# A four-layer cross-attention and feed-forward chain: extra constant products on TensorE, down products ten steps behind, and a split wait

## The chip, the cores and the metric

The kernel runs on one core of a Trainium2 chip. The metric is the time of one execution on the device in microseconds (us), as the median of several runs. Five engines work side by side, each through its own list of instructions in the order in which they were written: TensorE (PE, matrix products into PSUM), VectorE (DVE), ScalarE (ACT), GpSimd (POOL) and SyncE (SP, which here only starts DMAs). Semaphores order them against each other.

## The reference, cut to what matters

The input x is 4 batches of 256 tokens of width 256; a context of 4 times 64 tokens of width 64 is given too. Everything is float32, with a tolerance that makes the kernel split its operands into a high and a low float16 part in many places. Each layer adds a cross-attention and a feed-forward part to x, both of them on a normed x:

```
x = x + L0_xattn(layernorm(x), ctx)    # 16 heads of 16, causal, latent keys and values
x = x + L0_ffn(layernorm(x))           # one value projection, width 704, routed by a sign
x = x + L1_xattn(layernorm(x), ctx)    # folded head weights, rotated queries and keys
x = x + L1_ffn(layernorm(x))           # 64 experts of 64 (top 8) and a shared one
x = x + L2_xattn(layernorm(x), ctx)    # folded head weights, not rotated
x = x + L2_ffn(layernorm(x))           # self-attention, 8 experts of 176 (top 2), shared 704
x = x + L3_xattn(layernorm(x), ctx)    # as L0_xattn
x = x + L3_ffn(layernorm(x))           # 16 experts of 176 (top 4), shared 176
```

An expert part is `down(silu(gate(x)) * up(x))` times its gate; the kernel computes all experts for all tokens and multiplies by gates that are zero for those not chosen.

## The kernel before

The 1024 tokens are 8 tiles of 128 (`NT`). The stages follow each other in each engine's list in the order of the blocks at the end of `build`: latent attention 0, pre-work 0 and feed-forward 0, folded attention 1, router 1 and feed-forward 1, folded attention 2, self-attention with router 2 and feed-forward 2, latent attention 3, router 3 and feed-forward 3. No planner sets the order: it is written out by loops with offsets, and whatever PE waits for holds everything that follows it in PE's list.

**Constant products.** `pe_warm(n, free)` (L303, its product is L306) issues n products of the constant `ident_b` with the constant mask, 128 by 128 by 512 in bfloat16, into a PSUM bank that nothing reads. They have no effect on the result. The kernel before has them in several places already.

**Latent attention** (`pe_latent`, used for layers 0 and 3). Eight sets of heads run through scores (L419, mask L422), softmax on DVE and ACT, transposes (L430), values (L440), the transposed reciprocals (`inverse`, L449) and the output projection (`output`, L458), in a loop over m that has each step some turns behind the one before.

**Pre-work 0** (`pe_pre0`): transposes of z (L299), the folded projection (L1811), constants, then transposes of z2, which DVE writes in L1909.

**Folded attention 1** (`pe_rotated`): 48 units of queries (L1052 to L1054) and scores (L1066), and for each of the four batches four groups of transposes (L1076) and two outputs (L1084). After the last unit only the last batch's transposes and outputs are left; they wait for DVE, POOL (L1142) and ACT (L1115).

**Folded attention 2** (`pe_fold2`): eight pairs of heads, each with `folded` (L861), `chained` (L871), `values` (L883), `queries` (L890), `pe_fold_values` (L679) and `pe_keys2` (L922). Before the first stands the wait for the whole x of feed-forward 1 (`x_ready(pe, 2 * n)`).

**Self-attention** (`pe_self`): 32 steps; in each `turned` (L2236) transposes the exponentials of ACT (L2313) after waiting for them (`s.p`) and for DVE's copy of the turned block before (`s.pt`, L2329), then come scores two steps ahead, and the values. `project` (L2267) ends each group of four.

**Feed-forward** (`pe_ffn`, `act_ffn`, `dve_ffn`, `pool_ffn`, `sp_ffn`): the hidden width goes in steps, two for each tile of 128 columns (512 tokens each). In a step PE computes gate and up, six products each (L1450 to L1452); ACT takes the tanh, DVE forms the product into `m_b`, POOL multiplies the gate rows in (L1697), ACT and DVE split the product in high and low (L1604, L1651), and `LAG` steps later PE's `down` (L1495 to L1497, twelve products) takes it. `LAG` is 8, and it is also the number of slots of `m_b`. In the last `LAG` steps there are only down products left (`in_order`). The gate values come from the router: DVE ends them in L1997, PE transposes them (`gates_turned`, L1482) in step 3, ACT copies them in its step 4, SP writes them to memory and reads them back as rows (`m_g`). The weight tiles come by SP through two buffers each; a down tile is split by `act_dn_hi` and `dve_dn_lo`.

## Time and profile before

| what | value |
|---|---|
| median of 3 runs | 1262.36 us |
| the 3 runs | 1260.95, 1262.36, 4173.52 us |
| the profiled execution | 1260.15 us |
| its span | 1258.0 us |
| mean granted clock of TensorE in it | 0.981 |
| instructions in it | 21685 |

The span is the time from the first to the last instruction that the profile holds; the 2.15 us around it belong to the execution but to no row. One of the three runs took 4173.52 us; the other two lie 0.8 and 2.2 us above the profiled execution. In the rows, the granted clock is given as a share of full speed: 1.00 is 2.4 GHz, 0.50 is 1.2 GHz.

### The profile page before, as it was taken

To read this page: it belongs to the slowest core of one execution; us is meant where nothing else is said; L and a number is where in the kernel's file an instruction comes from. 1 tells how busy PE (TensorE), PEld (TensorE's weight loads), DVE (VectorE), ACT (ScalarE), POOL (GpSimd) and SP (SyncE) were. 2 spreads that over 40 slices of the span, in tenths; PEclk is the share of its full clock that TensorE was granted. 3 is DMA by queue.
4 is the path that set the end of the run, shared out by engine and by line. 5 is a ranking of instruction groups with operands and counts; after the bars stand their busy time and mean duration, and the time that the engine had idled before them with its cause. 6 is when DMAs were issued, how large, how long until landed. Compare 5 with 4: busy or idle time off the path is not lost.

```text
span 1258.0 us, 21685 instructions
## 1 busy us (share of the span) xinstructions
PE 1172.4 (93%) x8429; PEld 770.3 (61%) x8429; DVE 922.1 (73%) x1718; ACT 507.8 (40%) x1141; POOL 395.2 (31%) x397
## 2 busy tenths in 40 slices
PE   6988999999889999999999988889999988899998
PEld 3664657999645556565666745554666665455556
DVE  3677976767567777778757797887778576677777
ACT  3433361111124333333453336653334343555554
POOL 1450124666305333334102340002533142433331
PEclk9799999999999999999999999999999989999999
DMA  4040132000055444445140000002433100443441
GB/s 148 1 160 18 39 124 75 1 1 2 1 195 155 118 117 118 117 118 137 53 178 1 1 17 2 2 2 72 140 118 118 56 18 1 124 118 117 118 127 63
DMA packets 41541, 97.17 MB, mean 77 GB/s; under 512 B 5446, under 2 KB 18246, under 8 KB 39392
## 3 DMA queue, kind: packets, MB, share of 16 engines
q1 hardware_dynamic: 41440, 95.79, 25.0%
q8 instruction: 67, 1.10, 0.4%
q14 instruction: 34, 0.28, 0.1%
HBM read 94.35 MB, written 1.42 MB: 76 GB/s over the span
## 4 chain that ended last, share of the span: by engine, by line
PE 74%; DVE 16%; ACT 4%; issue 2%; DMA 2%; POOL 1%; SPq 0%; DVEq 0%; ACTq 0%; POOLq 0%
PE PS L1450 9%; PE PS L1451 9%; PE PS L1452 9%; PE PS L1495 5%; PE PS L1497 5%; PE PS L1496 4%; PE PS L1066 3%; PE PS L1084 2%; PE PS L1261 2%; PE PS L306 2%; ACT arena L2313 2%; PE PS L1052 2%; PE PS L1054 2%; PE PS L1053 2%; DVE arena L1651 2%
## 5 line engine op out<-in xcount | busy, mean ns | idle before, releaser
L1697 POOL TENSOR_TENSOR arena<-arena,m_g 128x512 f32<-128x512 f32 x142 | 198.3, 1417 | 361.2 <-DMA m_g<-gate_rows 314.8
L1450 PE MATMUL PS<-arena 128*128 128x512 f16 x608 | 231.5, 381 | 2.9 <-DVE arena L1637 2.4
L1451 PE MATMUL PS<-arena 128*128 128x512 f16 x608 | 231.3, 380 | 0.0
L1452 PE MATMUL PS<-arena 128*128 128x512 f16 x608 | 231.0, 380 | 0.0
L1495 PE MATMUL PS<-arena 128*128 128x256 f16 x608 | 165.9, 273 | 8.0 <-DVE arena L1651 6.6
L1497 PE MATMUL PS<-arena 128*128 128x256 f16 x608 | 165.8, 273 | 0.0
L1496 PE MATMUL PS<-arena 128*128 128x256 f16 x608 | 165.7, 273 | 0.0
L1594 ACT ACTIVATE arena<-PS 128x512 f32<-128x512 f32 x112 | 66.8, 597 | 229.2 <-PE PS L1452 227.5
L1640 DVE SCALAR_TENSOR_TENSOR arena<-arena,PS 128x512 f32<-128x512 f32 x112 | 76.9, 687 | 80.6 <-ACT arena L1594 78.8
L1651 DVE TENSOR_TENSOR arena<-arena 128x512 f16<-128x512 f32 x142 | 132.0, 931 | 2.9 <-ACT arena L1604 2.8
L1452 PEld LDWEIGHTS PS<-arena 128*128 128x128 f16 x608 | 59.7, 98 | 72.3 <-issue 1.1
L1450 PEld LDWEIGHTS PS<-arena 128*128 128x128 f16 x608 | 59.7, 98 | 62.7 <-DVE arena L1637 2.9
L1451 PEld LDWEIGHTS PS<-arena 128*128 128x128 f16 x608 | 59.7, 98 | 57.7 <-issue 0.6
L1135 POOL TENSOR_TENSOR arena<-arena 128x256 f32<-128x256 f32 x96 | 67.7, 728 | 79.2 <-DVE arena L1165 79.1
L1604 ACT ACTIVATE arena<-arena 128x512 f16<-128x512 f32 x142 | 87.6, 618 | 5.3 <-PE PS L1497 4.2
L1643 DVE TENSOR_TENSOR arena<-arena,PS 128x512 f32<-128x512 f32 x112 | 77.1, 688 | 12.2 <-DVE arena L1640 0.5
L1495 PEld LDWEIGHTS PS<-arena 128*128 128x128 f16 x608 | 59.4, 98 | 38.5 <-issue 10.2
L1539 DVE SCALAR_TENSOR_TENSOR arena<-w_stage,arena 128x512 f16<-128x512 f32 x80 | 79.2, 992 | 4.9 <-ACT arena L1534 4.9
L1496 PEld LDWEIGHTS PS<-arena 128*128 128x128 f16 x608 | 59.5, 98 | 17.0
L1497 PEld LDWEIGHTS PS<-arena 128*128 128x128 f16 x608 | 59.5, 98 | 6.9
L2313 ACT ACTIVATE arena<-PS,arena 128x128 f32<-128x128 f32 (+1 forms) x128 | 52.1, 422 | 20.4 <-DVE arena L2085 19.9
L1637 DVE TENSOR_TENSOR arena<-arena,PS 128x512 f32<-128x512 f32 x44 | 30.2, 686 | 37.5 <-PE PS L1452 37.2
(282 smaller groups left out, 2250.5 us busy)
## 6 DMA issues: line engine op xcount, KB each, us to landing
w_stage<-in_up SPq DMA_DIRECT2D x80, 256.0 KB, 2.8
m_g<-gate_rows SPq DMA_DIRECT2D x70, 256.0 KB, 4.2
arena<-in_heads SPq DMA_DIRECT2D x16, 1088.0 KB, 5.5
w_stage<-in_down SPq DMA_DIRECT2D x80, 128.0 KB, 4.0
m_g<-gate_rows SPq DMA_DIRECT2D x17, 512.0 KB, 4.1
m_g<-gate_rows SPq DMA_DIRECT2D x6, 448.0 KB, 4.0
m_g<-gate_rows SPq DMA_DIRECT2D x6, 384.0 KB, 4.0
m_g<-gate_rows SPq DMA_DIRECT2D x6, 320.0 KB, 4.5
```

The costliest lines, as they stand in the source:

```text
L1450: pe.matmul(to, w_hi, x_hi, start=(k == 0), stop=False)
L1451: pe.matmul(to, w_lo, x_hi, start=False, stop=False)
L1452: ins = pe.matmul(to, w_hi, x_lo, start=False, stop=(k == KT - 1))
L1495: pe.matmul(to, h_hi, w_hi, start=(c == 0 and i % 2 == 0), stop=False)
L1496: pe.matmul(to, h_hi, w_lo, start=False, stop=False)
L1497: ins = pe.matmul(to, h_lo, w_hi, start=False, stop=(last and i % 2 == 1))
L1539: nc.vector.scalar_tensor_tensor(up_w[:, c % 2, 1, :], up_in[:, c % 2, :], SPLIT, up_w[:, c % 2, 0, :], ALU.mult, ALU.subtract).then_inc(s ...
L1604: act.activation(hid_part(n, 0, st), m_b[:, st % LAG, :], ACT.Copy).then_inc(s.hi, 1)
L1643: dve.tensor_tensor(m_b[:, st % LAG, :], a, u_ps, ALU.mult).then_inc(s.prod, 1)
L1651: dve.tensor_tensor(hid_part(n, 1, st), m_b[:, st % LAG, :], hid_part(n, 0, st), ALU.subtract).then_inc(s.lo, 1)
L1697: pool.tensor_tensor(p, p, m_g[:, st // 2 % 2, st % 2, :], ALU.mult).then_inc(s.c, 1)
L2313: ins = act.activation(sa_p[:, t % 2, e, a * keys:(a + 1) * keys], PS[:, score_banks(t), a * keys:(a + 1) * keys][:, e, :], ACT.Exp, bias= ...
```

## The change

It consists of these edits. `LAG` becomes 10. In latent attention 4, 5 and 3 constant products come ahead of the loop and in its steps m = 2 and m = 3; `inverse(b)` comes behind the wait and the 4 constants that followed it; behind the last `inverse` come 6 constants (layer 0) or 16 (layer 3). In folded attention 2 the products of `folded(0)` come first, then a wait for x tile 5 alone, the first `pe_fold_values`, 4 constants; the wait for the whole x comes behind `chained(0)`, and 6 constants and the old wait go. At the end of folded attention 1, 3, 3, 11 and 3 constants come ahead of the last four groups of transposes, and 9 become 6 ahead of the output. In feed-forward 1 the gates are transposed in step 4 in place of 3, behind 5 constants, and ACT copies them in step 5; a down tile is no longer split for the first of two due steps where that one is odd. In pre-work 0, 13 constants become 28. In self-attention the wait for `s.pt` comes first, then 3 constants (t = 2, 6, 10, ..., 30) or 4 (t = 1 and 4), then the wait for `s.p`; 6 more stand ahead of the last `project`.

```diff
@@ -34,7 +34,7 @@
 UNDOWN = 1.0 / (HID * SPLIT)
 UP_W, DN_W = 4 * P, D
-LAG = 8
+LAG = 10
 HIDS = 4
 RING = 4
@@ -466,7 +466,10 @@
             scores(0)
             projected(1, 1)
+            pe_warm(4, LAT_Y)
             for m in range(1, SETS + 3):
+                if m in (2, 3):
+                    pe_warm(5 if m == 2 else 3, LAT_Y)
                 if m % 2 and m >= 3:
                     for q in range(QT):
@@ -480,11 +483,13 @@
                 if m % 2 and m >= 3:
                     b = (m - 3) // 2
-                    inverse(b)
                     if b < B - 1:
                         if n or b:
                             pe.wait_ge(soft.x, NT * n + 2 * b)
                         pe_warm(4, LAT_Y)
+                    inverse(b)
+                    if b == B - 1:
+                        pe_warm(16 if n else 6, LAT_BANK[0])
                 if m % 2 == 0 and m >= 4:
                     output((m - 4) // 2, 1)
@@ -897,13 +902,18 @@
                     ins.then_inc(ln.xT_ps, 1)
 
-            pe.wait_ge(*heads_loaded(2, 0))
+            folded(0)
+            x_ready(pe, 4, 5)
             pe_fold_values(6, 0).then_inc(s.e_ps, 1)
+            pe_warm(4, 0)
             for q in range(PAIRS):
-                folded(q)
+                if q:
+                    folded(q)
                 if q:
                     pe_keys2(q - 1)
                 chained(q)
+                if q == 0:
+                    x_ready(pe, 4)
                 values(q)
                 queries(q)
@@ -1011,8 +1021,6 @@
                 pe_rotated()
             else:
-                pe_warm(6, 3)
-                x_ready(pe, 2 * n)
                 pe_fold2()
                 pe_plain()
@@ -1092,11 +1100,13 @@
                 for e in range(4):
                     if at_turn(g, TURN_AT[e]) is not None:
+                        if g >= UNITS:
+                            pe_warm((3, 3, 11, 3)[e], 4)
                         transposed(at_turn(g, TURN_AT[e]), e)
                 for q in range(QT):
                     if at_turn(g, OUT_AT[q]) is not None:
                         if g >= UNITS and q == 0:
-                            pe_warm(9, 4)
+                            pe_warm(6, 4)
                         output(at_turn(g, OUT_AT[q]), q)
 
@@ -1372,6 +1382,9 @@
         def slot_load(s, kind, c):
             return {"up": (s.up0, s.up1), "dn": (s.dn0, s.dn1)}[kind][c % 2]
+
+        def gates_at(n):
+            return 4 if n == 1 else 3
 
         def gated(n, st):
@@ -1477,6 +1490,8 @@
 
             def gates_turned():
+                if n == 1:
+                    pe_warm(5, 6)
                 pe.wait_ge(s.parts, n)
                 for i in range(NT):
@@ -1519,7 +1534,7 @@
                 if st == 0 and n:
                     pe_logits(n, 1)
-                if st == 3 and f.gated:
+                if st == gates_at(n) and f.gated:
                     gates_turned()
                 if st == LAG and f.gated:
@@ -1608,13 +1623,14 @@
             for st in range(f.steps + LAG - 2):
                 c, h, due = st // 2, st % 2, finished(n, st)
-                if st == 4 and f.gated:
+                if st == gates_at(n) + 1 and f.gated:
                     act.wait_ge(s.gates_ps, n)
                     to_hid = HID * 0.5 * UNSPLIT * (1.0 if f.first else UNSPLIT)
                                    scale=to_hid).then_inc(s.gates, 1)
                 if len(due) == 2:
-                    act_dn_hi(n, due[0] // 2)
+                    if due[0] % 2 == 0:
+                        act_dn_hi(n, due[0] // 2)
                     high(due[0])
                 if begun <= st < f.steps:
@@ -1656,7 +1672,8 @@
                 c, h, due = st // 2, st % 2, finished(n, st)
                 if len(due) == 2:
-                    dve_dn_lo(n, due[0] // 2)
+                    if due[0] % 2 == 0:
+                        dve_dn_lo(n, due[0] // 2)
                     low(due[0])
                 if begun <= st < f.steps:
@@ -1812,7 +1829,7 @@
                 if i % 2:
                     ins.then_inc(s.y_ps, 1)
-            pe_warm(13, 3)
+            pe_warm(28, 3)
             pe_transpose_tiles(z, s.z2, 0, s.z2T_ps, BY_HALF)
             pe_warm(5, 4)
@@ -2227,9 +2244,11 @@
             def turned(t):
                 b, q, j0, keys = sa_part(t)
-                pe.wait_ge(s.p, t + 1)
                 if t:
                     pe.wait_ge(s.pt, t)
+                    if t % SA_OF_Q == 2 or t in (1, 4):
+                        pe_warm(3 if t % SA_OF_Q == 2 else 4, 2)
+                pe.wait_ge(s.p, t + 1)
                 for e in range(2):
                     for a in range(2):
@@ -2281,6 +2300,7 @@
             values(SA_STEPS - 2)
             sums_transposed(B * QT - 1)
+            pe_warm(6, 2)
             project(B * QT - 1)
 
```

## Rows read from the trace of the kernel before

**Rows 1.** The page: busy time by engine, and the chain that ended last.
```profile
PE 1172.4 (93%) x8429; PEld 770.3 (61%) x8429; DVE 922.1 (73%) x1718; ACT 507.8 (40%) x1141; POOL 395.2 (31%) x397
...
PE 74%; DVE 16%; ACT 4%; issue 2%; DMA 2%; POOL 1%; SPq 0%; DVEq 0%; ACTq 0%; POOLq 0%
```

**Rows 2.** Stretches: span, busy of PE, PEld, DVE, ACT, POOL, PE clock, DMA, GB/s.
```profile
32.60:49.70 17.10, 15.10 (x103) 11.46 (x102) 10.60 (x17) 7.66 (x13) 8.07 (x14) 0.50 0.01 1
100.60:104.60 4.00, 3.55 (x17) 3.51 (x18) 3.72 (x12) 2.37 (x6) 0.01 (x1) 0.57 0.00 0
336.50:340.00 3.50, 3.40 (x11) 1.76 (x12) 2.30 (x6) 1.59 (x3) 0.00 (x0) 0.51 0.00 0
367.30:370.90 3.60, 3.00 (x12) 2.26 (x13) 1.13 (x3) 0.99 (x1) 0.00 (x0) 0.53 0.25 74
752.40:756.00 3.60, 3.58 (x15) 1.31 (x16) 3.56 (x8) 0.11 (x1) 0.00 (x0) 0.58 0.00 0
1012.50:1023.00 10.50, 9.81 (x73) 7.33 (x74) 6.91 (x12) 4.62 (x8) 4.47 (x8) 0.52 0.10 27
1053.30:1056.80 3.50, 3.50 (x15) 2.95 (x14) 2.12 (x7) 0.59 (x2) 0.00 (x0) 0.51 0.02 5
1090.50:1094.10 3.60, 3.60 (x14) 1.58 (x12) 1.87 (x3) 1.06 (x3) 1.94 (x3) 0.55 0.93 255
```

**Rows 3.** PE's waits over the span: us in total, times, longest us.
```profile
PE PS L458 <- DVE arena L591: 7.1, 6, 4.2
...
PE PS L1495 <- DVE arena L1651: 6.6, 10, 2.0
```

**Rows 4.** Timeline of PE, constant products: start us, us, instruction, count.
```profile
47.54 1.91 PE L306 MATMUL PS<-causal_b,ident_b 128*128 128x512 bf16 x4
...
93.93 2.97 PE L306 MATMUL PS<-causal_b,ident_b 128*128 128x512 bf16 x13
```

**Rows 5.** Timeline of PE in latent attention 0 and 3; in brackets idle before, and releaser.
```profile
35.31 1.11 PE L430 MATMUL PS<-ident,arena 128*128 128x128 f32 x4 [1.32 <-ACT arena L520]
36.36 2.08 PE L419 MATMUL PS<-arena 32*128 32x128 f32 x16
...
50.92 1.16 PE L419 MATMUL PS<-arena 32*128 32x128 f32 x16
...
61.25 1.16 PE L419 MATMUL PS<-arena 32*128 32x128 f32 x16
...
1010.53 1.16 PE L419 MATMUL PS<-arena 32*128 32x128 f32 x16
...
1024.15 1.16 PE L419 MATMUL PS<-arena 32*128 32x128 f32 x16
...
1052.40 2.92 PE L458 MATMUL PS<-arena 128*128 128x256 f32 x8 [4.21 <-DVE arena L591]
```

**Rows 6.** Timeline of PE, then of DVE, where pre-work 0 ends.
```profile
101.05 3.58 PE L299 MATMUL PS<-ident,arena 128*128 128x128 f32 x16 [4.15 <-DVE arena L1909]
...
100.64 2.19 DVE L1909 TENSOR_SCALAR arena<-arena,rms_r 128x256 f32<-128x256 f32 x8 [1.76 <-POOL rms_r L1836]
```

**Rows 7.** Timeline of PE at the end of folded attention 1.
```profile
335.17 0.66 PE L1076 MATMUL PS<-ident,arena 128*128 128x128 f32 x4 [2.94 <-POOL arena L1142]
...
337.48 3.32 PE L306 MATMUL PS<-causal_b,ident_b 128*128 128x512 bf16 x9
```

**Rows 8.** Timeline of PE where feed-forward 1 and 3 begin.
```profile
367.90 1.97 PE L1482 MATMUL PS<-ident,arena 128*65 128x128 f32 x8 [4.45 <-DVE arena L1997]
...
384.30 0.27 PE L1495 MATMUL PS<-arena 128*128 128x256 f16 x1 [1.03 <-DVE arena L1651]
...
1089.63 0.27 PE L1495 MATMUL PS<-arena 128*128 128x256 f16 x1 [2.04 <-DVE arena L1651]
```

**Rows 9.** Timeline of PE where folded attention 2 begins.
```profile
620.13 1.10 PE L871 MATMUL PS<-arena 96*128 96x64 f32 x8 [0.47 <-ACT arena L957]
```

**Rows 10.** Timeline of PE in self-attention, steps 10 and 14.
```profile
784.68 0.66 PE L2236 MATMUL PS<-ident,arena 128*128 128x128 f32 x4 [0.78 <-ACT arena L2313]
...
795.72 1.06 PE L2236 MATMUL PS<-ident,arena 128*128 128x128 f32 x8 [0.96 <-DVE arena L2329]
```

## The prediction

> **What bounds the kernel now.** I read the page first: TensorE (PE) is busy for 93% of the span and holds 74% of the chain that ended last [rows 1]. So what counts is what PE does, how fast its clock lets it, and the 86 us (1258.0 - 1172.4) in which it stands. Then I cut the span into slices of half a microsecond and looked for a granted clock under 1.00. It is low in eight stretches [rows 2]; the share of a stretch at the half level (1.2 GHz) is twice what is missing from 1.00: 17.1, 3.4, 3.4, 3.4, 3.0, 10.1, 3.4 and 3.2 us, 47 us in all. PE is busy for 45.5 us of them, so a clock that never fell would give back at most 23 us. Last I read PE's waits [rows 3] and its timeline around each place that the diff touches. Ahead of each low stretch PE stood for microseconds or did short work between waits: 4.15 us before 101.05 [rows 6], 2.94 before 335.17 [rows 7], 4.45 before 367.90 and 2.04 before 1089.63 [rows 8], 4.21 before 1052.40, and 1.32 before 35.31 [rows 5].
>
> The sum is made against the profiled execution, 1260.15 us, which is 2.2 us under the median; the next run of before is 0.8 us above it. I add 1.5 us at the end.
>
> **Constant products.** Thirteen at full clock take 2.97 us and four at half clock 1.91; the last one of each has to drain, so one more costs 0.216 us or 0.427 us (the difference of neighbours' starts) [rows 4]. One that stands in a wait is free if it ends before the wait does; if not, all that is behind it in PE's list is later by the rest.
>
> *Latent attention, layers 0 and 3.* At full clock the loop needs 10.33 us for two steps of m (50.92 to 61.25). The two before took 14.56 in layer 0 (36.36 to 50.92) and 13.62 in layer 3 (1010.53 to 1024.15) [rows 5], most of it at half clock [rows 2]. If the added products hold the clock, 4.2 and 3.3 us go. The work of the steps is the same, so the row nearest to the new stretch is the loop at full clock; a few tenths are lost again by the `inverse` that now stands behind four constants (0.86 us, most of it in a wait that it had for POOL: an estimate). The five products at m = 2 are 1.08 us and fit in the 1.32 us before 35.31. I take -4.0 + 0.2 and -3.3 + 0.3. If the clock falls all the same, the twelve cost 12 x 0.427 = 5.1 us against some 3.3 us of waits: +1.8 us for each layer. In layer 3 the last wait is 4.21 us [rows 5]; 16 products are 3.46 us and are hidden, the transposes and outputs of 1053.3 to 1056.8 are at half clock now [rows 2], and half of 3.4 us is 1.7: I take -1.5 (0 to -1.7). The six in layer 0 (1.3 us) stand in a wait of the same kind (one of six, 7.1 us in all [rows 3]): 0.
>
> *Pre-work 0.* 28 products from 93.93 end at 93.93 + 28 x 0.216 = 100.0, within PE's wait until 101.05 [rows 4, 6]. The sixteen transposes behind it take 3.58 us at half clock; at full clock they would follow DVE, whose eight writes end at 102.83 [rows 6], and end some 1.4 us earlier. DVE then still has its splitting to do, which PE's next products wait for, so less than that arrives: -0.9 (0 to -1.5).
>
> *End of folded attention 1.* The eleven products are 2.37 us in the wait of 2.94 us [rows 7]: hidden. The three ahead of the first group stand in no wait and delay the chain by up to 0.65 us; part of it is lost in waits of ACT, I take 0.25. Behind, six at full clock (1.3 us) replace nine that took 3.32 us at half clock, and a group of transposes speeds up by 0.4 us: 0.25 - 2.0 - 0.4 = -2.1. If the clock falls earlier, eleven cost 4.7 us in a wait of 2.94: up to +2.4.
>
> *Self-attention.* 8 x 3 + 2 x 4 = 32 products, 6.9 us. In step 10 the wait is for ACT (0.78 us) and the copy of the block before is done by its start: three products (0.65 us) are hidden. In step 14 the wait of 0.96 us is for that copy itself (L2329), and the constants stand behind it: 0.65 us late [rows 10]. Steps 10, 18 and 26 are of the first kind, 14, 22 and 30 of the second, and I count 2 and 6 with these. A later wait of PE for ACT takes up a part; I take 0.4 for each of the five: +2.0 (0 to +6.9). The clock was 1.00 in this stretch, so there is nothing to win. The six ahead of the last `project`: 0.
>
> **Down products ten steps behind.** The number of products is the same. What changes is the start: ten steps of up products (12 x 0.216 = 2.6 us each) run before the first down product, 5.2 us more than with eight. In feed-forward 3 PE waited 2.04 us for the first down operand, because the gate rows arrive late, and the clock then fell for 3.2 us [rows 2, 8]: 2.0 + 1.6 = -3.6 (0 to -3.7). Feed-forward 2 has a small wait of the same kind: of the 6.6 us in ten waits for L1651 [rows 3], 3.1 us are named here, and I take 0.7 of the rest: -0.7. At the ends ten down products run in a row in place of eight, and with them the down tiles have to come one after the other through two buffers: +0.3 (0 to +2). Feed-forward 0 has only 11 steps; nearly all its down products now come behind all up products, where DVE's splitting and its work for the routing set the pace: +0.5 (-0.5 to +2).
>
> *Feed-forward 1* also has its gates a step later. PE stands 4.45 us, until DVE's gates are there, and the transposes take 1.97 us, mostly at half clock [rows 8]. Now the products of step 4 come first; they need the next weight tile, which DVE splits only behind the gates, so PE stands 0.6 us longer. Then come step 4 (the clock low until 370.9 as before [rows 2]), five constants (1.08 us) in no wait at all, and the transposes at full clock, 1.0 in place of 1.8 us: 0.6 + 1.08 - 0.8 + 0.4 for the products that take the half clock in the transposes' place = +1.3. The 1.03 us before 384.30 [rows 8] should go: the transposes end some 4.4 us later (about 374.3 in place of 369.9), and the first down product comes 5.2 + 1.3 us later. But the margin is thin, I take +0.8 (0 to +3).
>
> **Second fold.** Six constants (1.3 us), the wait for x and the folded values came before the products of `folded(0)`; ACT's copy of these ended the wait at 620.13 [rows 9]. Now `folded(0)` runs while DVE still adds x, and ACT's copies follow some 0.8 us earlier: -0.8 (0 to -1.3).
>
> **Sum:** latent attention -3.8 - 3.0 - 1.5, pre-work -0.9, folded attention 1 -2.1, self-attention +2.0, feed-forward 0 to 3 +0.5 + 0.8 - 0.7 - 3.6, ends +0.3, second fold -0.8: -12.8. 1260.15 - 12.8 + 1.5 = 1248.9 us.
>
> **The skill against it.** The clock is at the half level for 47 of 1258 us [rows 2], 3.7% of the span, and giving it all back would be 1.9%. The Trainium skill ("TensorE: Matmul & The Clock Gate", "What's actually happening") says that the ramp costs under 1% of a typical kernel's span and that the number of slow products changes from run to run. By its 1% the clock part of my sum (4.2 + 3.3 + 1.5 + 0.9 + 2.4 + 1.6 = 13.9 us) would be 12.6 us at most, and the result 1250.2. The rows show more than that for this kernel. The second half of the rule is rival B, whose price comes from rows.
>
> **The rivals.**
> A. *The constants are not hidden in self-attention and in the latent loops.* For it: step 14's wait is DVE's [rows 10], and PE's queue is in order. Price: self-attention 32 x 0.216 = 6.9; latent attention +1.8 + 1.8 at half clock; folded attention 1 +2.4; feed-forward 1 +1.6; with the gains that don't hang on it (-0.9 - 1.5 - 0.8 - 4.3 + 0.8): +7.8, so 1269 us. It decides from the point where a constant outlasts the wait: 1.32 us holds six at full clock and three at half. Against it: most waits are longer than what is put in.
> B. *The clock falls elsewhere.* The stretch at 752.4 lies in code that isn't changed ahead of it, and whether a wait lowers the clock depends on more than its length: 4.21 us and 2.04 us did [rows 5, 8], the 1.03 us before 384.30 did not [rows 2, 8], so a wait in between may do so once it has moved. If the latent loops fall back for half of their length (+3.6) and two new stretches of 3.4 us come (+3.4), the result is 1256 us.
> C. *More than I count.* No cost in self-attention, none at the ends, and the stretches at 367.3 and 752.4 go too (-3.1): 1249 - 2 - 3.1 - 1.3 = 1242.5 us.
> D. *LAG does nothing for the starts.* If POOL and the gate rows set the pace, the wait before the first down product only moves: without -3.6, -0.7 and the 1.03 us, 1254 us.
>
> **How the numbers follow.** Forecast 0.45, A 0.12, B 0.22, C 0.11, D 0.10. Its own range is 1244 to 1253; with B, C and D whole and part of A 1240 to 1262. A measurement of this kernel can tell 2% (25 us) from no change: under 1237 us there would have to be more than all the clock gives, over 1287 us more than A. Faster by over 2%: 0.04, slower: 0.02, within: 0.94.
>
> **What would show it.** Right: the granted clock 1.00 between 28 and 60 us, at 101, 337, in both ends of latent attention 3 and behind the first down product of feed-forward 3; no wait before the first down products; two steps of the latent loop in 10 to 11 us from m = 2; self-attention 2 us longer; the gates of feed-forward 1 transposed some 6 us later. Wrong: half-clock stretches in the latent loops (B), constants with DVE and ACT idle beside them in self-attention (A), a wait before the first down product (D).

## The result, and the profile after

| | median (fastest to slowest) | ratio to before, 95% interval |
|---|---|---|
| before, 6 runs beside it | 1260.81 us (1259.71 to 4173.52) | |
| after, 6 runs | 1252.97 us (1250.47 to 1255.29) | 0.9933 (0.9911 to 0.9954) |
| after, profiled | 1252.46 us, span 1250.4 us, mean granted clock 0.996 | |

One run of before (4173.52 us) and one of e7 below (6432.05 us) stand far outside the others; the ratios and e7's range leave them out.

The forecast was 1249 us with a range of 1240 to 1262 us, a gain of 1.1% on the median before; measured is a gain of 0.7%, with the time near the upper end of the forecast's own narrow range (1244 to 1253). The sum itself (1247.4 us for the profiled execution) missed by 5.1 us, and that is two errors against each other: the four feed-forwards came out 9.8 us worse than in the sum, all the rest 4.7 us better. That the time lies so near the forecast is in part luck.

Line numbers in the rows of a run are those of its own kernel. In the changed kernel the gate product L1450 is L1463, the down product L1495 is L1510, the DVE split of the product, L1651 (L1653 in feed-forward 0), is L1667 (L1669), the product L1637 is L1653, and the split of an up tile, L1539, is L1554. The page of the changed kernel, the lines of [rows 1]:

```profile
PE 1179.2 (94%) x8519; PEld 767.1 (61%) x8548; DVE 918.0 (73%) x1718; ACT 505.3 (40%) x1141; POOL 391.4 (31%) x397
...
PE 72%; DVE 16%; DMA 3%; ACT 3%; issue 3%; POOL 2%; SPq 1%; DVEq 0%; ACTq 0%; POOLq 0%
```

PE is busy for 6.8 us more in a span that is 7.6 us shorter: the added constants are in it, and the waits and the half clock are what went. Stretches of the changed kernel, with the columns of [rows 2]:

```profile
28.00:60.00 32.00, 28.53 (x299) 20.02 (x303) 24.65 (x42) 17.39 (x31) 16.67 (x28) 1.00 0.01 2
361.00:368.00 7.00, 5.30 (x12) 1.94 (x14) 2.26 (x6) 1.11 (x2) 0.00 (x0) 0.51 0.13 37
752.40:756.00 3.60, 2.79 (x20) 1.20 (x18) 2.46 (x6) 2.51 (x11) 0.00 (x0) 1.00 0.00 0
1012.00:1023.00 11.00, 10.07 (x115) 7.43 (x112) 8.48 (x16) 5.94 (x11) 5.93 (x11) 1.00 0.01 3
1064.00:1068.00 4.00, 3.66 (x13) 1.69 (x14) 2.27 (x4) 1.28 (x4) 0.00 (x0) 0.57 0.29 66
```

Of the 47.8 us at half clock ahead of the last products, 10.2 are left (6.8 at 361 and 3.4 at 1064). The latent loops run at 1.00 throughout. PE's timeline in them, at the end of latent attention 3, at the end of pre-work 0 and at the end of folded attention 1 (the places of [rows 5], [rows 6] and [rows 7]):

```profile
34.43 1.16 PE L419 MATMUL PS<-arena 32*128 32x128 f32 x16
...
45.15 1.16 PE L419 MATMUL PS<-arena 32*128 32x128 f32 x16
...
1045.88 2.00 PE L458 MATMUL PS<-arena 128*128 128x256 f32 x8 [0.76 <-DVE arena L596]
...
88.38 5.99 PE L306 MATMUL PS<-causal_b,ident_b 128*128 128x512 bf16 x27
95.29 2.27 PE L299 MATMUL PS<-ident,arena 128*128 128x128 f32 x16 [0.91 <-DVE arena L1926]
...
328.01 2.54 PE L306 MATMUL PS<-causal_b,ident_b 128*128 128x512 bf16 x11
...
332.37 1.46 PE L306 MATMUL PS<-causal_b,ident_b 128*128 128x512 bf16 x6
```

Two steps of the loop that took 14.56 us take 10.72 (34.43 to 45.15). The wait of 4.21 us before the last outputs holds 16 constants and 0.76 us of idle time, and the eight outputs take 2.00 us in place of 2.92. The sixteen transposes of pre-work 0 take 2.27 us in place of 3.58.

PE's waits over the span, with the columns of [rows 3]:

```profile
PE PS L1463 <- DVE arena L1554: 6.1, 1, 6.1
PE PS L1510 <- DVE arena L1667: 6.0, 11, 1.2
PE PS L306 <- DVE arena L2349: 5.5, 9, 1.1
PE PS L458 <- DVE arena L596: 4.5, 8, 0.8
...
PE PS L1463 <- DVE arena L1653: 2.9, 2, 2.4
```

The down products (L1510, L1495 before) still wait 6.0 us for L1667, against 6.6 us, now in eleven waits: no long one, and hardly less in all. In feed-forward 1 one wait of 6.1 us stands where 4.45 us stood [rows 8]. PE's timeline there:

```profile
362.58 0.61 PE L1463 MATMUL PS<-arena 128*128 128x512 f16 x1 [6.10 <-DVE arena L1554]
...
368.01 1.03 PE L306 MATMUL PS<-causal_b,ident_b 128*128 128x512 bf16 x4
368.88 1.04 PE L1497 MATMUL PS<-ident,arena 128*65 128x128 f32 x8
...
390.57 0.28 PE L1510 MATMUL PS<-arena 128*128 128x256 f16 x1 [1.21 <-DVE arena L1667]
```

Step 4's products now come first. They wait for DVE's split of the third weight tile, and PE's list holds nothing else: the five constants stand behind this wait, not in it. The clock falls, all twelve products of step 4 run at half clock (362.58 to 367.9, 5.3 us in place of 2.6), and the constants come when there is nothing left to cover. DVE's timeline shows why the wait is longer than the 0.6 us that the forecast added: the split follows the sums of the gates in its list.

```profile
359.48 0.68 DVE L2010 TENSOR_TENSOR arena<-arena 128x512 f32<-128x512 f32 x1
360.20 0.69 DVE L2011 TENSOR_REDUCE arena<-arena 128x8 f32<-128x512 f32 x1
...
361.84 0.68 DVE L1554 SCALAR_TENSOR_TENSOR arena<-w_stage,arena 128x512 f16<-128x512 f32 x1
```

The lengths of the stages, each from its first to its last product in the two traces, in us against before:

| stage | predicted | after | the same kernel profiled again |
|---|---|---|---|
| latent attention 0 up to the loop; the loop | 0; -3.8 | -1.3; -4.5 | -0.8; -4.4 |
| pre-work 0 | -0.9 | -1.1 | -1.1 |
| feed-forward 0 | +0.5 | +2.2 | +2.2 |
| end of folded attention 1 | -2.1 | -2.3 | -2.3 |
| feed-forward 1 | +0.8 | +5.4 | +2.0 |
| second fold | -0.8 | -1.0 | -1.0 |
| self-attention | +2.0 | -0.3 | +1.4 |
| feed-forward 2 | -0.7 | -0.8 | +0.7 |
| latent attention 3 | -4.5 | -4.3 | -4.4 |
| feed-forward 3 | -3.6 | +0.3 | -0.3 |

(The predicted +0.3 for the ends is not placed.) The last column is e5 below. The same program differs by 3.4 us in feed-forward 1, where the clock was low for 3.4 us in place of 6.8 and PE stood 1.8 us less, and by 1.7 us in self-attention, where a stretch of 3.4 us at 748 is in the one trace and not in the other. So the length of a single stage is good to the clock's luck in it. The end of folded attention 1, pre-work 0, the second fold, feed-forward 0 and latent attention 3, which have no low stretch, agree to 0.1 us. Feed-forward 2 has none either and differs by 1.5 us: there it is waits, 0.3 us for L1667 in the one trace and 1.9 us in the other.

### The profile page after: what moved, and what is told of

It reads as the page before. It is cut to its first block, busy times and chain, and to the rows that moved or that the text cites. A ratio compares the mean times of both kernels' runs of the same rounds, so it can differ in the third digit from the quotient of the medians.

```text
span 1250.4 us, 21883 instructions
## 1 busy us (share of the span) xinstructions
PE 1179.2 (94%) x8519; PEld 767.1 (61%) x8548; DVE 918.0 (73%) x1718; ACT 505.3 (40%) x1141; POOL 391.4 (31%) x397
## 4 chain that ended last, share of the span: by engine, by line
PE 72%; DVE 16%; DMA 3%; ACT 3%; issue 3%; POOL 2%; SPq 1%; DVEq 0%; ACTq 0%; POOLq 0%
PE PS L1463 8%; PE PS L1465 8%; PE PS L1464 8%; PE PS L1510 5%; PE PS L1512 5%; PE PS L1511 5%; PE PS L1074 3%; PE PS L1092 2%; PE PS L306 2%; PE PS L1271 2%; DMA w_stage<-in_up 2%; PE PS L1060 2%; PE PS L1062 2%; PE PS L1061 2%; PE PS L2255 1%
## 5 line engine op out<-in xcount | busy, mean ns | idle before, releaser
L1714 POOL TENSOR_TENSOR arena<-arena,m_g 128x512 f32<-128x512 f32 x142 | 194.8, 1391 | 359.9 <-DMA m_g<-gate_rows 351.0
L1463 PE MATMUL PS<-arena 128*128 128x512 f16 x608 | 232.1, 382 | 9.6 <-DVE arena L1554 6.1
L1510 PE MATMUL PS<-arena 128*128 128x256 f16 x608 | 165.9, 273 | 9.1 <-DVE arena L1667 6.0
L1667 DVE TENSOR_TENSOR arena<-arena 128x512 f16<-128x512 f32 x142 | 125.4, 887 | 2.2 <-ACT arena L1619 1.8
L1463 PEld LDWEIGHTS PS<-arena 128*128 128x128 f16 x608 | 59.7, 98 | 71.4 <-DVE arena L1554 6.6
L1659 DVE TENSOR_TENSOR arena<-arena,PS 128x512 f32<-128x512 f32 x112 | 77.0, 688 | 13.7 <-PE PS L1465 1.5
L1554 DVE SCALAR_TENSOR_TENSOR arena<-w_stage,arena 128x512 f16<-128x512 f32 x80 | 81.6, 1022 | 7.0 <-ACT arena L1549 7.0
L1510 PEld LDWEIGHTS PS<-arena 128*128 128x128 f16 x608 | 59.4, 98 | 39.1 <-DVE arena L1667 10.7
L306 PE MATMUL PS<-causal_b,ident_b 128*128 128x512 bf16 x235 | 57.6, 379 | 7.3 <-DVE arena L2349 5.5
```

The lines of the kernel that those rows point to most:

```text
L306: nc.tensor.matmul(PS[:, free, :], ident_b[:], mask_lat, start=True, stop=True)
L1463: pe.matmul(to, w_hi, x_hi, start=(k == 0), stop=False)
L1510: pe.matmul(to, h_hi, w_hi, start=(c == 0 and i % 2 == 0), stop=False)
L1554: nc.vector.scalar_tensor_tensor(up_w[:, c % 2, 1, :], up_in[:, c % 2, :], SPLIT, up_w[:, c % 2, 0, :], ALU.mult, ALU.subtract).then_inc(s ...
L1659: dve.tensor_tensor(m_b[:, st % LAG, :], a, u_ps, ALU.mult).then_inc(s.prod, 1)
L1667: dve.tensor_tensor(hid_part(n, 1, st), m_b[:, st % LAG, :], hid_part(n, 0, st), ALU.subtract).then_inc(s.lo, 1)
```

## Experiments

All ratios are against before on the same chip. "Half clock" is the time at 1.2 GHz ahead of the last products, from the granted clock of half-microsecond stretches. The other columns are the stage's length against before's trace.

| run | median us (range) | ratio (95%) | half clock | ffn 0 | ffn 1 | ffn 2 | ffn 3 |
|---|---|---|---|---|---|---|---|
| before | | | 47.8 | | | | |
| e1 | 1248.95 (1247.8-1249.9) | 0.9879 (.9857-.9902) | 10.2 | 0.0 | +2.6 | 0.0 | +0.4 |
| e2 | 1249.47 (1247.9-1250.8) | 0.9883 (.9860-.9907) | 6.8 | +2.2 | +0.7 | -0.1 | -1.5 |
| e3 | 1252.17 (1248.8-1255.6) | 0.9902 (.9875-.9930) | 17.1 | 0.0 | +5.2 | +0.6 | +1.5 |
| e4 | 1263.43 (1260.8-1271.2) | 1.0003 (.9983-1.0023) | 47.8 | +2.2 | -1.7 | +0.8 | +3.0 |
| e5 | 1251.71 (1250.3-1253.1) | 0.9918 (.9899-.9936) | 10.2 | +2.2 | +2.0 | +0.7 | -0.3 |
| e6 | 1254.54 (1252.9-1256.7) | 0.9942 (.9923-.9961) | 17.1 | +2.2 | +2.8 | +1.1 | +1.8 |
| e7 | 1264.44 (1255.0-1267.3) | 1.0014 (.9993-1.0036) | 37.5 | +2.2 | +3.5 | -0.6 | +4.4 |
| e8 | 1245.65 (1244.6-1247.6) | 0.9872 (.9851-.9892) | 6.8 | 0.0 | +0.1 | +0.6 | 0.0 |
| e9 | 1247.61 (1244.0-1250.5) | 0.9876 (.9849-.9903) | 6.8 | +2.2 | -1.4 | +1.8 | +0.5 |
| e10 | 1244.58 (1243.3-1246.1) | 0.9856 (.9826-.9886) | 3.4 | 0.0 | -1.5 | -0.8 | -0.3 |
| e11 | 1247.60 (1245.5-1248.7) | 0.9877 (.9850-.9904) | 3.4 | +2.2 | -1.0 | -0.7 | -1.3 |
| e12 | 1245.85 (1244.9-1246.7) | 0.9865 (.9835-.9894) | 3.4 | 0.0 | +0.7 | +1.0 | -2.2 |

(Before's medians on the three chips were 1263.9, 1262.1 and 1263.8 us.)

### The feed-forward edits taken back, alone and together (e1 to e4)

**e1**: the changed kernel with all of its feed-forward edits taken back. **e2**: only the gates' step and its constants back. **e3**: only the distance back. **e4**: the kernel before with the distance of ten alone (and, as the change has it, a down tile split once and not twice where two steps are due).

The distance (e1, e3), then the gates (e1, e2):

```diff
-LAG = 10
+LAG = 8
```

```diff
-            return 4 if n == 1 else 3
+            return 3
...
-                if n == 1:
-                    pe_warm(5, 6)
```

> The changed kernel with LAG back at 8 and the gates of feed-forward 1 back in step 3 without the five constants; all other constants and the split wait stay. Theory (the feed-forward edits cost what the constants win): feed-forward 0 takes 2.2 us less than in the changed kernel, feed-forward 1 some 4 to 5 less, feed-forward 2 0.8 more, so 1246 us (1244 to 1248). Rival (the feed-forward stages lost by the place where the clock fell and by a late weight tile, whatever LAG is): the wait ahead of step 4 of feed-forward 1 stays at 6 us with 6.8 us at half clock, and the time stays at 1251 to 1253 us.

> The changed kernel with LAG 10, but the gates of feed-forward 1 in step 3 again and without the five constants ahead of them. Theory (the gate step costs by itself: the constants in no wait, and twelve products at half clock where transposes were): feed-forward 1 is 2 to 3 us shorter, 1250 us. Rival (the gate step is free, the loss is LAG's): within 1 us of the changed kernel, 1252 to 1254 us.

> The changed kernel with LAG 8, the gates of feed-forward 1 still in step 4 behind five constants. Theory: feed-forward 0 takes back its 2.2 us, but in feed-forward 1 the gate rows now come too late for a first down product after eight steps: PE waits 4 to 6 us there, so 1252 to 1255 us. Rival (the gates have slack enough): the wait stays at 1 us and the time is 1248 to 1250 us.

> The kernel before with LAG 10 alone. Theory (LAG alone wins nothing): feed-forward 0 +2.2 us, feed-forward 1 about 0 (its 1 us wait moves to the second down product, where the up tile arrives late), feed-forward 2 -0.8, feed-forward 3 between -1.6 and 0: 1260 to 1262 us. Rival (my forecast: the waits ahead of the first down products go): -3.5 us, 1257 us.

Measured: e1 and e2 lie 2 to 4 us under the changed kernel's two medians (1252.97 and 1251.71), 0.4 to 0.5% by the ratios, and do not differ from each other. e1 is 1 us over the range expected. So the constants and the second fold give 15 us on their own (1263.88 - 1248.95), 1.2%, and with the feed-forward edits 0.7 and 0.8% are left: they take a third or more of it away.

The distance of ten alone does nothing for the time (e4, 1.0003); in place of the gain of up to 1.6 us expected for feed-forward 3, e4's trace has a loss of 3.0. The traces divide the rest. Feed-forward 0 is 2.16 or 2.17 us longer in each of the eight traces with ten steps there and within 0.01 us of before in each of the five with eight. PE's waits at its end, of the changed kernel:

```profile
131.86 0.27 PE L1510 MATMUL PS<-arena 128*128 128x256 f16 x1 [0.79 <-DVE arena L1669]
133.84 0.27 PE L1510 MATMUL PS<-arena 128*128 128x256 f16 x1 [0.51 <-DVE arena L1669]
135.82 0.27 PE L1510 MATMUL PS<-arena 128*128 128x256 f16 x1 [0.51 <-DVE arena L1669]
137.80 0.27 PE L1510 MATMUL PS<-arena 128*128 128x256 f16 x1 [0.51 <-DVE arena L1669]
```

Each down step follows the one before by 1.98 us, DVE's pace with the routing in it, where PE would need 1.5. There are two more such steps behind the last up product: from there to the end it is 18.7 us in place of 14.8, and ahead of it the stage is only 1.7 us shorter. In feed-forward 1 the distance gains 1.5 to 1.9 us, since its wait before the first down product goes (e1 against e2, e8 against e9). The two cancel.

The gates a step later cost 2.6 us with eight steps (e3 against e1, both with 6.8 us of half clock there) and up to 4.7 us with ten (the changed kernel against e2). In e3 PE waits 1.76 us before the first down product, not the 4 to 6 us expected.

Feed-forward 1 is 2.6 us longer than before in e1 too, where none of its edits is left. The wait for the gates is 5.22 us there in place of 4.45 [rows 8], and the low stretch behind it 6.8 us in place of 3.4:

```profile
359.89 1.97 PE L1495 MATMUL PS<-ident,arena 128*65 128x128 f32 x8 [5.22 <-DVE arena L2012]
```

The gates' transposes begin 17.0 us after the first product of the stage (16.9 to 17.1 in all six traces with the gates in step 3 behind the changed end of folded attention 1), 16.2 in before: PE is 2.3 us quicker through that end, and 0.8 us of it is lost again in this wait. So a part of the changed kernel's +5.4 us hangs on no edit of this stage. Why the low stretch is twice as long is not shown; in e5, behind a wait of 5.71 us, it is 3.4 us again.

### The changed kernel again, and without its constants (e5 to e7)

**e5** is the changed kernel. **e6** leaves out those of self-attention, **e7** those added in the two latent stages.

```diff
-                    if t % SA_OF_Q == 2 or t in (1, 4):
-                        pe_warm(3 if t % SA_OF_Q == 2 else 4, 2)
...
-            pe_warm(6, 2)
```

```diff
-            pe_warm(4, LAT_Y)
...
-                if m in (2, 3):
-                    pe_warm(5 if m == 2 else 3, LAT_Y)
...
-                    if b == B - 1:
-                        pe_warm(16 if n else 6, LAT_BANK[0])
```

> The changed kernel itself once more, on the chip of the next three runs, as their ground. Every theory: 0.993 of the time before (1252 to 1255 us), feed-forward 0 2.2 us longer than before, feed-forward 1 about 5.4 us longer, half clock for some 7 us ahead of the products of feed-forward 1's step 4 and for some 3 us in feed-forward 3.

> The changed kernel without the 38 constant products in self-attention. Theory one (constants that fill waits keep the clock up and pay wherever the clock would fall): self-attention loses the 1.4 us which the constants cost there, but the half-clock stretch at its start (before: 752.4 to 756, some 1.6 us of loss) comes back, net within 0.5 us either way of the changed kernel. Rival (they are pure cost there): 1.4 us faster, with no half-clock stretch. Second rival (they hold the clock up further on): the clock falls in several further places of self-attention or of the stages behind it, 2 to 4 us slower.

> The changed kernel without the constants added in the latent stages 0 and 3 (the changed order of the inverse stays). Theory one (the constants there are what took the half-clock stretches of 17 and 10 us away): latent 0 is 5 to 6 us longer than in the changed kernel, latent 3 3 to 4 us longer, with half clock in both, 9 us in all, so 1261 to 1263 us, equal to the kernel before. Rival (the order of the inverse, or chance, took them away): latent stages as in the changed kernel, within 1 us.

Measured, e5: the time repeats (1251.71 us), but feed-forward 1 is 2.0 us longer than before and not 5.4, with 3.4 us at half clock and not 7.

e7: the half clock is back in both loops, at the end of latent attention 3 (1052), and at 1072 and 1099 as well. Stretches of e7, with the columns of [rows 2]:

```profile
34.50:49.00 14.50, 13.65 (x96) 10.30 (x96) 7.91 (x13) 5.82 (x11) 6.81 (x11) 0.53 0.01 2
1011.00:1018.00 7.00, 6.31 (x61) 4.79 (x60) 4.55 (x8) 3.49 (x6) 4.13 (x8) 0.51 0.11 40
...
1099.50:1103.50 4.00, 4.00 (x17) 1.94 (x16) 3.79 (x3) 1.18 (x3) 3.22 (x2) 0.57 0.53 156
```

The order of `inverse` is as in the changed kernel, so it is not what helped. The median is 12.7 us above e5, more than the 9 us expected. In the traces the latent stages account for 9.2 us; 4.7 more lie in feed-forward 3, which had no edit, and 1.4 in feed-forward 1, where the low stretch was 6.8 us long in place of 3.4; self-attention and feed-forward 2 are 3.0 us shorter together. Not all of that is the clock. From the first to the last product of feed-forward 3 PE stands 5.3 us in e5, 7.8 us in e7, 8.6 us in e4 (+3.0) and 5.7 us before, and the half clock is 3.4, 6.8, 3.4 and 3.4 us. Why these waits are longer in e4 and e7 is not settled.

e6: 2.8 us slower than e5, and their six runs hardly touch. Its mean granted clocks are 0.990 to 0.996 against 0.995 to 0.999. Self-attention itself is 0.8 us shorter without the 38 constants (both traces have the low stretch at its start), which is their price. Against before, whose trace has that stretch too, it is 1.4 us longer in e5 and still 0.7 us in e6; no run says where the 0.7 us come from. The time is that of the second rival, but the mechanism is not shown: in the traces e6 has 0.7 us more in feed-forward 1, which lies ahead of self-attention, and one more low stretch (1091 to 1095), over 240 us behind the last of these constants.

### Constants where the clock still fell (e8, e12)

**e8** is e1 with constants in the two waits behind which e1's clock still fell (cuts against the changed kernel); in **e12** those of feed-forward 1 are 36 transposes of the unit matrix.

In `gates_turned` ahead of the wait for `s.parts`, and in the steps' loop ahead of the wait before the second product:

```diff
                 if n == 1:
-                    pe_warm(5, 6)
+                    pe_warm(18, 6)
...
+                if st == 3 and n == 3:
+                    pe_warm(9, 7)
```

In e12 in place of the first:

```diff
-                    pe_warm(18, 6)
+                    for i in range(36):
+                        pe.transpose(PS[:, 6, i % 4 * P:(i % 4 + 1) * P], ident[:], ident[:])
```

> The changed kernel with the down products eight steps behind and the second gates in step 3, as before, and with constants of some 4 us in each of two places where the trace of the changed kernel still shows half clock: ahead of the wait for the parts of the transposed input in feed-forward 1, and ahead of the wait before step 3's second product in feed-forward 3. Theory one (each wait that PE fills keeps the clock, and the products behind it run at full speed): both stretches at about 360 and 1064 go, feed-forward 1 gains 3 to 3.5 us on the run that has eight steps and gates in step 3, feed-forward 3 about 1.5 us: 1244 to 1246 us. Rival (the clock falls for another reason, such as work that comes ahead of the wait): the stretches stay or move by a few us, and the time is 1249 us or up to 1 us more.

> The kernel of e8_fills with the 18 constant products of feed-forward 1 replaced by 36 transposes of the unit matrix of some 4 us together. Theory one (any work of the array holds the clock): no half clock there, feed-forward 1 and the whole as in e8, 1245.7 us within 1. Rival (transposes do not hold the clock up): half clock for some 7 us at about 360, feed-forward 1 some 2.5 us longer, 1248 us.

Measured, e8: 1245.65 us, as theory one had it, and 6 us under the changed kernel on the same chip (e5). PE's timeline of e8 in both places:

```profile
354.25 4.05 PE L306 MATMUL PS<-causal_b,ident_b 128*128 128x512 bf16 x18
...
1057.33 2.11 PE L306 MATMUL PS<-causal_b,ident_b 128*128 128x512 bf16 x9
1059.86 0.39 PE L1463 MATMUL PS<-arena 128*128 128x512 f16 x1 [0.43 <-DVE arena L1655]
...
1078.06 0.31 PE L1510 MATMUL PS<-arena 128*128 128x256 f16 x1 [2.78 <-DVE arena L1669]
```

and stretches of e8:

```profile
342.70:375.00 32.30, 29.64 (x167) 14.28 (x163) 22.95 (x56) 11.06 (x21) 4.30 (x4) 1.00 0.55 198
...
1047.00:1078.00 31.00, 27.85 (x163) 13.15 (x160) 22.59 (x60) 14.29 (x27) 6.02 (x4) 1.00 0.25 78
1078.00:1082.00 4.00, 3.94 (x17) 2.37 (x18) 3.90 (x4) 1.15 (x2) 3.37 (x3) 0.57 0.66 206
```

Both filled waits keep the clock at 1.00, and it falls behind the next unfilled one, of 2.78 us, which is why feed-forward 3 gains nothing in this trace. Feed-forward 1 gained 2.5 us on e1, not 3 to 3.5: of e1's 6.8 us at half clock the first 1.5 lie in the wait itself, 5.3 us of busy time are left, and half of that is 2.6. The gates (17.05 us after the first product) and the first down product's wait (1.54 us, e1 1.45) stay where they were.

e12: 1245.85 us, as theory one had it. The transposes end as the constants did, and the clock stays at 1.00 behind them.

```profile
354.29 4.09 PE L1495 MATMUL PS<-ident 128*128 128x128 f32 x36
359.83 1.09 PE L1498 MATMUL PS<-ident,arena 128*65 128x128 f32 x8 [1.45 <-DVE arena L2017]
```

Here 4.1 us of transposes in float32 hold the clock as well as 4.05 us of products do; the rival falls. In e12 the clock held in feed-forward 3 too, at the same wait of 2.78 us behind which it fell in e8, and that stage is 2.2 us shorter: luck of the kind e5 shows.

### The distance and the gates with the clock held up (e9 to e11)

**e9** is e8 with `LAG` 10. **e10** is e9 with the distance of eight in feed-forward 0 alone. **e11** is e9 with the gates in step 4, as in the change, and 24 constants ahead of step 4's wait in place of the five behind it.

e10 (`lag(n)` in place of `LAG` everywhere but in the slots of `m_b`), then e11:

```diff
+        def lag(n):
+            return LAG if n else 8
```

```diff
+                if st == 4 and n == 1:
+                    pe_warm(24, 6)
                 if h == 0:
                     pe.wait_ge(s.up_lo, f.tiles0 + c + 1)
```

> The kernel of e8_fills with the down products ten steps behind instead of eight; nothing else differs. Theory one (the distance of ten steps takes away the wait before the first down product where there is one, and adds the splitting of two more steps on VectorE behind the last product where VectorE is the last to finish): feed-forward 0 2.2 us longer, feed-forward 1 about 1.5 us shorter (its wait of 1.54 us goes), feed-forward 3 about 2.8 us shorter (its wait of 2.78 us and the half-clock stretch behind it go), feed-forward 2 within 0.7 us: 1243 to 1244.5 us, 1.5 to 2.5 us under e8. Rival (in the three later feed-forwards the split of two more steps at the end costs as much as in the first): each loses 2 us at its end, 1248 to 1252 us.

> The kernel of e9_lag10_fills with the distance of eight steps in feed-forward 0 alone. Theory one: the 2.2 us of feed-forward 0 come back and nothing else changes, 1241 to 1242.5 us, the fastest of the study. Rival (the gain at the end of feed-forward 0 turns into a wait behind it): feed-forward 0 ends 2 us earlier and the next stage starts no earlier, 1243 to 1244.5 us.

> The kernel of e9_lag10_fills with the second gates of feed-forward 1 in step 4, as the change has them, and the constants (24) ahead of step 4's wait instead. Theory one (the later gates cost what they do by the half clock of step 4's products, some 2.6 us up to the first down product, and by the loads of the sixth tile that stand behind the gate rows in SyncE's queue, some 2 us): with the clock held up the first part goes and the second stays, so feed-forward 1 is about 1.5 to 2 us longer than in e9 and shows an idle time of over 1 us behind a load of a tile of up weights some 30 us into it. Rival (all of it is the clock): as e9 within 0.5 us. Second rival (all of it is the place): 4 to 5 us longer than e9.

Measured, e9: 1247.61 us, 3 us over the range expected, which for the whole is no gain on e8 (the intervals overlap). Feed-forward 0 (+2.16) and feed-forward 1 (-1.5 against e8) came as said. Feed-forward 2 did not (+1.8, e8 +0.6), nor did feed-forward 3: its wait of 2.78 us became one of 2.04, not none.

```profile
1085.05 0.27 PE L1510 MATMUL PS<-arena 128*128 128x256 f16 x1 [2.04 <-DVE arena L1669]
```

e10: feed-forward 0 is back to 0.0, the next stage starts that much earlier (its rival falls), and feed-forward 1 keeps its gain. Its median is the lowest of the study, but 1.1 us under e8 with intervals that overlap, and 2 us over the range expected. It beats both kernels: 1243.3 to 1246.1 us against 1250.5 to 1255.3 for the changed one.

e11: feed-forward 1 is 0.4 us longer than in e9, so the rival holds: what the later gates cost was nearly all the clock and the five constants in no wait (1.1 us), and the loads behind the gate rows cost nothing of their own.

```profile
357.83 5.13 PE L306 MATMUL PS<-causal_b,ident_b 128*128 128x512 bf16 x23
363.53 0.39 PE L1463 MATMUL PS<-arena 128*128 128x512 f16 x1 [0.57 <-DVE arena L1556]
```

The wait of 6.1 us is there as before, but full of constants; step 4's products run at full clock, and the wait of 1.21 us behind the sixth tile's load is not in this trace.

## Why the prediction was right or wrong

**Constants in waits: right.** Latent attention, pre-work 0, the end of folded attention 1 and the second fold were to give 12.1 us; the trace has 14.5, of which 1.3 come before the loop and change from run to run. e1 shows that they are the whole gain (15 us), and e7 that those of the latent stages are most of it (9.2 us in those stages). Pre-work 0, the end of folded attention 1 and the second fold were not taken back one by one; their gains are read from the traces and are alike to 0.1 us in all twelve that have them. Rival A (1269 us) fell: the clock was 1.00 beside the constants, and all 38 of self-attention cost 0.8 us. Only the five of feed-forward 1, which stand in no wait, cost their full 1.1 us.

**Self-attention, +2.0: the size was off.** Where the low stretch ahead of it is there as before, the stage is 1.4 us longer (e5), 0.8 us of it the constants (e6). The -0.3 of the changed kernel's trace is luck: the stretch, which lies ahead of every constant added to this stage, is missing in it. It was said that there is nothing to win; e6 is 2.8 us slower, at lower mean clocks, by a way that is not shown.

**Feed-forward 0, +0.5: the size was off.** The step named the mechanism, DVE setting the pace behind the last up product, and bounded it at +2; it is +2.16, on the bound and beyond. Two more steps at DVE's pace (2 x 1.98 us), less the 1.7 us that go ahead of them, was the sum to make.

**Feed-forward 1, +0.8: the step failed in three places.** "Now the products of step 4 come first ... so PE stands 0.6 us longer" measured 1.65 us (6.10 against 4.45). And "the clock low until 370.9 as before" took the low stretch for a thing of fixed place and length. It follows the wait: here it ran over all twelve products of step 4, which take 0.43 us each in it in place of 0.22. e11 shows that this and the constants in no wait were nearly the whole price of the later gates. Third, the sum did not carry on what the stages ahead had won: PE comes to the wait for the gates earlier and stands longer, and the low stretch was 6.8 us in place of 3.4; that is +2.6 in e1, without any edit in this stage.

**Feed-forward 3, -3.6: the step failed, and rival D was right here** in that the wait only moves. "PE waited 2.04 us for the first down operand, because the gate rows arrive late" gave a wrong reason. After, the waits are still 2.02 us, in three parts:

```profile
1085.63 0.39 PE L1463 MATMUL PS<-arena 128*128 128x512 f16 x1 [0.51 <-DVE arena L1653]
1087.73 0.27 PE L1510 MATMUL PS<-arena 128*128 128x256 f16 x1 [0.63 <-DVE arena L1667]
...
1092.67 0.28 PE L1510 MATMUL PS<-arena 128*128 128x256 f16 x1 [0.88 <-DVE arena L1667]
```

The trace of before, POOL and then DVE around the first down product (the split L1651 of step 0, and the same line late in the stage), shows the reason:

```profile
1084.56 6.06 POOL L1697 TENSOR_TENSOR arena<-arena,m_g 128x512 f32<-128x512 f32 x4 [27.05 <-DMA m_g<-gate_rows]
...
1087.74 1.75 DVE L1651 TENSOR_TENSOR arena<-arena 128x512 f16<-128x512 f32 x1
...
1247.34 0.68 DVE L1651 TENSOR_TENSOR arena<-arena 128x512 f16<-128x512 f32 x1
```

The rows arrive late, but what PE waits for is DVE, whose operations with both inputs in SBUF take up to 1.75 us in place of 0.68 while POOL works off its four late products. POOL has the same work with ten steps, so DVE is late by the same 2 us, wherever PE is. This agrees with the Trainium skill ("SBUF — State Buffer", "SBUF: two separate sides"): VectorE with two SBUF inputs and GpSimd share a port pair, and the one that comes second stands until the other's instruction is done. No run here took POOL's work away, so the cause of DVE's lateness is read, not tried. That the distance does not help is tried: over the whole stage PE stands 4.2 and 3.8 us with eight steps (e8, e12) and 4.2, 3.9 and 4.2 us with ten (e9 to e11). The low stretch behind the wait did go at 1090, and another came at 1064, behind the wait of 2.37 us that had not lowered the clock before: rival B in small. That a stretch would go with its wait and none come was the other half of -3.6.

**Feed-forward 2 and latent attention 3** came as said (-0.8 for -0.7, -4.3 for -4.5), the former by luck: it is +0.7 in e5 and 0.0 in e1, with eight steps.

**The Trainium skill's 1%** ("TensorE: Matmul & The Clock Gate", "What's actually happening"), that slow products cost under 1% of a span: with constants in only part of the waits 15 us of 1264 are back (e1), 1.2%, or 1.1% without the second fold's 1 us, and 1.3% in e8. The eight stretches of [rows 2] alone come to half of 45.5 us, 1.8% (an estimate). For this kernel it is more than the page has. Its other half, that the number of slow products changes from run to run, is what e5 shows.

## What to carry to other kernels

Put filler products into the wait itself, ahead of the instruction that waits in PE's list; behind it they are pure cost, and the clock has fallen. Expect a part of what a stage wins to end in the next wait. Before a group is moved past another, look at which of the two runs just behind the wait, because that one pays the half clock. A longer software distance shifts work behind the last producer, where the slower engine sets the pace: choose it for each stage, and ask first whether the wait is for a late start or for an engine that is behind with its work.

## What was not expected of the hardware

The clock differs between executions of one program: the changed kernel had 3.4 us or 6.8 us at 1.2 GHz behind the same wait (6.10 us, and 5.71 in e5), and a low stretch near the start of self-attention, beginning between 743 and 758, is in eight of the twelve experiments' traces and missing in four. The wait of 2.37 us in feed-forward 3 was followed by a low stretch in the changed kernel and not in the one before, the one of 2.78 us in e8 and not in e12. The spread goes with it, roughly: the runs of e8 lie within 3.1 us and those of e1 within 2.1, those of e4 and e7 within 10.4 and 12.3 us, but there are five or six of the one and eleven or twelve of the other, and e9's lie within 6.6 us.

A DVE operation with both inputs in SBUF takes 0.68 us alone and up to 1.75 us beside POOL's; the product that reads PSUM (L1637, 686 ns on average over feed-forward 3) keeps its time beside the same work.
